# Four convolution taps on VectorE, thirteen pooled key tiles and maxima by accumulators alone, in a two-layer attention kernel

## The reference

```python
g = clip(bn(conv1x1(l, w_inside)), 0, 6)
theta = l[:, :32]
f = einsum('niab,nicd->nabcd', theta, theta)
f = softmax(f.reshape(n, h * w, h, w), axis=1)
f = softmax(f.reshape(n, h * w, h * w), axis=2)
out = einsum('nabcd,nicd->niab', f, g) / h * w
out = bn(conv3x3_depthwise(out, w_dw)) + l
```

## Time and profile before

| | us |
|---|---|
| Median of 3 runs (5228.88 to 5233.55) | 5230.44 |
| Span of the profiled execution | 5229.7 |
| TensorE busy | 5201.4 (99%) |
| ScalarE busy | 5093.6 (97%) |
| GpSimd busy | 4435.3 (85%) |
| VectorE busy | 4411.4 (84%) |

### The profile page before, as it was taken

The page is one execution under the profiler, slowest core; times in us unless marked ns, Lnnn a source line. Parts: engine busy times, 40 slices in busy tenths (PEclk is TensorE's granted clock), DMA queues, the critical chain, the costliest instruction groups (busy, mean ns, idle before and its releaser), DMA issues.

```text
span 5229.7 us, 88157 instructions
## 1 busy us (share of the span) xinstructions
PE 5201.4 (99%) x32196; PEld 2524.0 (48%) x32196; DVE 4411.4 (84%) x8862; ACT 5093.6 (97%) x2949; POOL 4435.3 (85%) x1854
## 2 busy tenths in 40 slices
PE   9999999999999999999999999999999999999999
PEld 3333355444545444545454444545454545444544
DVE  8888888888888888888888888888888888888887
ACT  8888889999999999999999999999999999999998
POOL 7666655998888998888998998899888899888988
PEclk9999999999999999999999999999999999999999
DMA  8898852223222222223232223222222322222122
GB/s 161 169 185 168 164 104 46 48 55 64 55 63 54 55 63 63 63 63 63 63 63 54 47 52 64 59 61 60 48 60 63 63 63 63 63 63 55 43 42 49
DMA packets 226669, 380.19 MB, mean 73 GB/s; under 512 B 158086, under 2 KB 174527, under 8 KB 216128
## 3 DMA queue, kind: packets, MB, share of 16 engines
q1 hardware_dynamic: 225136, 373.67, 34.5%
q10 hardware_dynamic: 1104, 0.89, 0.1%
HBM read 258.82 MB, written 102.74 MB: 69 GB/s over the span
## 4 chain that ended last, share of the span: by engine, by line
PE 83%; ACT 10%; issue 5%; DVE 2%; DMA 0%; SPq 0%; POOL 0%; DVEq 0%
PE at_AV L1302 35%; PE at_S L1261 21%; PE at_AV L1308 10%; ACT at_ring L1044 7%; PE l_TY L612 6%; PE l_TY L619 4%; PE l_SEL L601 3%; ACT at_ring L1050 3%; PE at_AV L1298 2%; DVE at_ring L1117 2%; PE at_AV L1273 0%; DVE at_GT L1177 0%; DVE at_ZACC L1220 0%; DMA l_X<-in_x 0%; DVE at_ACC L1210 0%
## 5 line engine op out<-in xcount | busy, mean ns | idle before, releaser
L1117 DVE TENSOR_SCALAR_CACHE_REDUCE at_ring<-at_S 128x1344 f32<-128x1344 f32 (+2 forms) x2352 | 2882.8, 1242 | 461.2 <-PE at_S L1261 444.3
L992 POOL TENSOR_TENSOR at_ZP<-at_ZP,at_ring 128x1568 f32<-128x1568 f32 x640 | 2268.5, 3581 | 144.4 <-ACT at_ring L1050 134.4
L1302 PE MATMUL at_AV<-at_ring,at_GT 128*64 128x392 f32 x12800 | 2300.3, 500 | 3.8 <-issue 3.7
L1044 ACT ACTIVATE at_ring<-at_ring,at_NM 128x3136 f32<-128x3136 f32 x784 | 2272.6, 2899 | 12.8 <-DVE at_NM L1126 11.8
L1050 ACT ACTIVATE at_ring<-at_ring,at_RZ 128x3136 f32<-128x3136 f32 x784 | 2274.0, 2901 | 0.0
L1302 PEld LDWEIGHTS at_AV<-at_ring,at_GT 128*64 128x64 f32 x12800 | 854.1, 137 | 1143.8 <-issue 1107.6
L1261 PE MATMUL at_S<-at_THM,at_THS 128*128 128x448 f32 x5376 | 1381.7, 387 | 11.6 <-DVE at_ring L1117 9.2
L1261 PEld LDWEIGHTS at_S<-at_THM,at_THS 128*128 128x128 f32 x5376 | 927.1, 188 | 631.6 <-DVE at_ring L1117 291.4
L1013 POOL TENSOR_TENSOR at_OUTB<-at_OUTB,at_ZB 128x1568 f32<-128x1568 f32 x246 | 878.1, 3570 | 16.8
L1308 PE MATMUL at_AV<-at_ring,at_ones 128*32 128x392 f32 x7168 | 676.9, 498 | 2.9 <-DVE at_ACC L1210 2.9
L567 DVE TENSOR_TENSOR l_U<-l_TY,l_XB 128x512 f32<-128x512 f32 x784 | 486.8, 683 | 86.0 <-PE l_TY L612 84.3
(11 more groups left out here) (91 smaller groups left out, 2491.4 us busy)
## 6 DMA issues: line engine op xcount, KB each, us to landing
at_THM<-hld SPq DMA_DIRECT2D x128, 392.0 KB, 6.2
at_THS<-hld SPq DMA_DIRECT2D x256, 192.0 KB, 4.0
l_X<-in_x SPq DMA_DIRECT2D x124, 392.0 KB, 7.2
at_CIN<-att SPq DMA_DIRECT2D x62, 406.0 KB, 7.5
at_ZB<-rzd SPq DMA_DIRECT2D x62, 406.0 KB, 7.8
yd<-l_YO SPq DMA_DIRECT2D x128, 196.0 KB, 5.4
att<-at_ACC SPq DMA_DIRECT2D x248, 98.0 KB
at_OUTB<-yd SPq DMA_DIRECT2D x62, 392.0 KB, 8.5
```

Of the source, the lines that this page charges most:

```text
L992: e.tensor_tensor(z, z, v, ALU.add).then_inc(g_add, 1)
L1044: e.activation(v, v, ACT.Exp, bias=NM[:, i:i + 1], accum_out=ZS[:, i:i + 1]).then_inc(a_p1, 1)
L1117: e.tensor_scalar(ring[:, s % RING, SC * a_:SC * b].rearrange("p (b w) -> p b w", w=SC), PS[:, k % 2, bank:bank + b - a_, 0:SC], 1.0, None ...
L1302: ins = e.matmul(dst[64 * j:64 * j + 64, 0:QC], GT[fl.n % 2][:, keys_of(fl.n, t), :], ring[:, slot, q:q + QC], start=(i == 0), stop=(i == ...
```

## The change

- Taps 0 to 3 of the nine leave GpSimd for VectorE, for all images but the last: `tap` is one `scalar_tensor_tensor` each, `OUTB + w * CIN`. The first waits for step 0 (new semaphore `g_sc`) and for `OUTB`'s load, each other for the one before. GpSimd's first sum (tap 4) waits for the four (`v_cv`). The planner gives a tap rank 3 and 1950 ns.
- Step 1 goes: the bias is added in the product of tap 4.
- `POOL_OF` goes from 2 to 3 in the first two groups: tiles 1 to 6, 8, 9, 12, 13, 16, 17 and 19 are pooled, 13 in all.
- `negmax` goes: the copies negate the scores and take a minimum, the second and third piece with the previous piece's result as second scalar, so the last one leaves the negated maximum in `NM`. Each waits for the one before. The first exponential has scale −1, and waits for `v_m`.

```diff
-POOL_OF = (2, 2, 2, 2, 2, 1, 0)
+POOL_OF = (3, 3, 2, 2, 2, 1, 0)
...
+TAPS = (0, 1, 2, 3)
...
-    conv = [(n, step) for n in range(n_img - 1) for step in range(20)]
+    conv = [(n, step) for n in range(n_img - 1) for step in range(20) if step == 0 or step > 1 and (step - 2) // 2 not in TAPS]
+    taps = [(n, v) for n in range(n_img - 1) for v in TAPS]
...
+        if taps:
+            cv.append((max(td, scaled.get(taps[0][0], inf) + LAT), 3, "tap"))
...
-            cg.append((max(tg, image_end.get(conv[0][0], inf) + 20000), 1, "conv"))
+            n, step = conv[0]
+            first = step == 3 + 2 * next(v for v in range(9) if v not in TAPS)
+            cg.append((max(tg, image_end.get(n, inf) + 20000, tapped.get(n, inf) + LAT if first else 0.0), 1, "conv"))
...
+            elif what == "tap":
+                n, v = taps.pop(0)
+                td = t + 1950
...
-                    link(e.tensor_tensor(CIN[:, :, 1:57], CIN[:, :, 1:57], ZB[:, :, :], ALU.mult))
-                elif step == 1:
-                    e.wait_ge(s_ob, 32 * (n + 1))
-                    link(e.tensor_scalar(OUTB[:, :], OUTB[:, :], 1.0, bq[:, 4:5], ALU.mult, ALU.add))
+                    e.tensor_tensor(CIN[:, :, 1:57], CIN[:, :, 1:57], ZB[:, :, :], ALU.mult).then_inc(g_sc, 1)
+                    e.wait_ge(g_sc, n + 1)
...
-                    link(e.tensor_scalar(T3, CIN[:, i:i + 28, j:j + 56], w9[:, v:v + 1], 0.0, ALU.mult, ALU.add))
+                    link(e.tensor_scalar(T3, CIN[:, i:i + 28, j:j + 56], w9[:, v:v + 1], bq[:, 4:5] if v == TAPS[-1] + 1 else 0.0,
+                                         ALU.mult, ALU.add))
...
+                    if v == TAPS[-1] + 1:
+                        e.wait_ge(v_cv, len(TAPS) * (n + 1))
...
-                e.wait_ge(v_nm, s + 1)
+                e.wait_ge(v_m, NP * (s + 1))
...
-                e.activation(v, v, ACT.Exp, bias=NM[:, i:i + 1], accum_out=ZS[:, i:i + 1]).then_inc(a_p1, 1)
+                e.activation(v, v, ACT.Exp, scale=-1.0, bias=NM[:, i:i + 1], accum_out=ZS[:, i:i + 1]).then_inc(a_p1, 1)
...
+                if c:
+                    e.wait_ge(v_m, m)
+                elif s >= 4:
+                    e.wait_ge(v_m, NP * (s - 3))
+                if s >= 4 and c == NP - 1:
+                    e.wait_ge(a_p1, s - 3)
+                least = NM[:, i:i + 1] if c == NP - 1 else MX[:, i, c:c + 1]
...
-                                PS[:, k % 2, bank:bank + b - a_, 0:SC], 1.0, None, ALU.mult, ALU.max,
-                                accum_out=MX[:, i, c:c + 1]).then_inc(v_m, 1)
...
-                e.tensor_reduce(NM[:, i:i + 1], MX[:, i, :], axis=AX.X, op=ALU.max, negate=True)\
-                 .then_inc(v_nm, 1)
+                                PS[:, k % 2, bank:bank + b - a_, 0:SC], -1.0, MX[:, i, c - 1:c] if c else None, ALU.mult, ALU.min,
+                                accum_out=least).then_inc(v_m, 1)
...
+            def tap(n, v):
+                i, j = divmod(v, 3)
+                if v == TAPS[0]:
+                    e.wait_ge(g_sc, n + 1)
+                    e.wait_ge(s_ob, 32 * (n + 1))
+                else:
+                    e.wait_ge(v_cv, len(TAPS) * n + TAPS.index(v))
+                O3 = OUTB[:, :].rearrange("p (r w) -> p r w", w=W)
+                e.scalar_tensor_tensor(out=O3, in0=CIN[:, i:i + 28, j:j + 56], scalar=w9[:, v:v + 1], in1=O3,
+                                       op0=ALU.mult, op1=ALU.add).then_inc(v_cv, 1)
```

More of the change, by code:

```diff
@@ L172, in plan @@
     adds = [(n, t, h) for n in range(n_img) for t in POOLED for h in range(2)]
-    conv = [(n, step) for n in range(n_img - 1) for step in range(20)]
+    conv = [(n, step) for n in range(n_img - 1) for step in range(20) if step == 0 or step > 1 and (step - 2) // 2 not in TAPS]
+    taps = [(n, v) for n in range(n_img - 1) for v in TAPS]
+    scaled, tapped = {}, {}
     inf = float("inf")
@@ L176, in plan @@
     pe, dve, pool = [], [], []
-    end_s, end_m, end_nm, end_a, end_r, end_p2, group_end, t_fill = {}, {}, {}, {}, {}, {}, {}, {}
+    end_s, end_m, end_a, end_r, end_p2, group_end, t_fill = {}, {}, {}, {}, {}, {}, {}
     end_add, summed, image_end = {}, {}, {}
     tp = ta = td = tg = 0.0
-    n_s = n_m = n_nm = n_r = n_ev = n_a = 0
+    n_s = n_m = n_r = n_ev = n_a = 0
     cur, at, mode = None, 0, 0
@@ L186, in units_at @@
         return end_add.get((f.n, POOLED[-1], f.j), inf) + LAT if t == SUM else 0.0
-    while n_a < 2 * total or main or cur is not None or n_ev < len(fills) or adds or conv:
+    while n_a < 2 * total or main or cur is not None or n_ev < len(fills) or adds or conv or taps:
         t_s = inf
@@ L218, in plan @@
             if n_a == 0:
-                t_a = max(ta, end_nm.get(0, inf) + LAT)
+                t_a = max(ta, end_m.get(NP - 1, inf) + LAT)
             elif n_a == 2 * total - 1:
@@ L222, in plan @@
             elif part == 1:
-                t_a = max(ta, end_nm.get(s + 1, inf) + LAT)
+                t_a = max(ta, end_m.get(NP * (s + 2) - 1, inf) + LAT)
             else:
@@ L228, in plan @@
         cv = []
-        if n_m < NP * total and n_m // NP == n_nm:
+        if n_m < NP * total:
             s = n_m // NP
@@ L237, in plan @@
             cv.append((max(td, end_s.get(piece(n_m)[3], inf) + LAT, free), 2, "M"))
-        elif n_nm < total:
-            cv.append((max(td, end_m[NP * n_nm + NP - 1] + LAT), 0, "nm"))
         if n_r < total:
@@ L304, in plan @@
                 n_m += 1
[L305 to L308, removed]
             elif what == "r":
@@ L312, in plan @@
                 n_r += 1
+            elif what == "tap":
+                n, v = taps.pop(0)
+                td = t + 1950
+                if v == TAPS[-1]:
+                    tapped[n] = td
+                dve.append(("tap", n, v))
             else:
@@ L328, in plan @@
                 tg = t + (3600 if step == 0 or step % 2 and step > 1 else 1620)
+                if step == 0:
+                    scaled[n] = tg
                 pool.append(("conv", n, step))
@@ L686, in build @@
         ZC = sb("ZC", [98, 32])
-        MX = sb("MX", [128, 4, NP])
+        MX = sb("MX", [128, 4, NP - 1])
         NM = sb("NM", [128, 4])
@@ L753, in build @@
         v_wt = sem("vwt")
-        v_nm = sem("vnm")
         v_fin = sem("vfin")
         v_m = sem("vm")
+        v_cv = sem("vcv")
+        g_sc = sem("gsc")
         v_r = sem("vr")
@@ L1061, in _ @@
             e.wait_ge(v_wt, 1)
-            e.wait_ge(g_w, 19 * (last - 1) + 1)
+            e.wait_ge(g_sc, last)
             for k, v in enumerate(HELPED):
@@ L1225, in first_tile @@
                     copy(m)
-                negmax(0)
             l0_vector(e, fold, first_tile)
-            acts = {"M": copy, "nm": negmax, "r": recip, "ev": evacuate}
+            acts = {"M": copy, "r": recip, "ev": evacuate, "tap": tap}
             for n in range(last):
@@ L1238, in _ @@
             acts["lz"] = last_shares
-            for what, *args in dve_order[NP + 1:]:
+            for what, *args in dve_order[NP:]:
                 acts[what](*args)
```

7 lines of the change are left out of this document (removed).

## The result

The changed kernel takes 5400.73 us in the median of four runs (5387.96 to 5412.32), against 5231.29 of the kernel before in the same comparison. The ratio is 1.0323, with an interval of 1.0310 to 1.0335. So it is 169 us slower; 57 were forecast, and the range ended at 5390. The profiled execution's span is 5400.3 us (before: 5229.7).

A forecast was written before the change was run, and what follows sets the result against it. ScalarE was taken to bound the attention stage, with VectorE having to feed it in time. 5229.7 − 4 (TensorE's relief) + 62 (ScalarE standing behind blocked taps) + 1 for the median gave 5288 us, range 5222 to 5390.

The forecast's parts named there:

- What bounds the kernel: Attention stage: ScalarE, 99.98% busy, sets a floor of 784 steps of 5.70 us, 4465 us, that TensorE's relief can't lower.
- TensorE's 87 us of relief: Row-sum matmuls dropped for newly pooled tiles: 2.7 us an image, hidden behind ScalarE, worth 0 to 6 us, taken as 4.
- The accumulators: Maxima taken in VectorE's copies instead of 784 reductions: load 4.89 us a tile, bounds 4.65 to 5.1.
- A tap by itself: One unblocked tap of 1568 elements on VectorE: 1.85 us, four of them 7.4 us an image.
- The standing: A VectorE tap meeting a GpSimd instruction that reads SBUF waits until it ends: 1.4 us a tap on average.
- Slack: Taps put VectorE 5 us behind per image; 3.0 us slack before ScalarE absorbs part, leaving 2 us, 62 in all.
- The upper end, 155 us: Worst end for the taps: each waits 1.79 us, 6.6 us behind against 1.6 of slack, over 31 images.
- The wait for the scaled image: First tap waits for GpSimd's scaling, moved from about 30 to 56 us by two extra pooled tiles; costed at nothing.
- the rival without it: Scaling planned before tile 6, VectorE stands for it: 7 us an image, 217 in all, about 5445 us; chance 0.10.
- at full clock: Expected sign in the profile after: TensorE shows waits for evacuations while its clock stays full; no size given.
- The taps hide: Rival: GpSimd's idle times and scores running ahead hide VectorE's taps, slack exceeds 5 us: 5225 to 5232 us; chance 0.27.
- TensorE's relief pays: Rival: ScalarE only follows TensorE's pace, so 87 us go: 5143 us, or 5220 at best with ScalarE's floor; chance 0.10.

The follow-up runs named there:

- experiments 4: Kernel before with only the accumulator maxima and the bias in a scaled copy; all nine taps on GpSimd, 11 pooled tiles: 5236.32 us (1.0009).
- experiment 7: Changed kernel with the four VectorE taps left out and planned at price 0, so no order is shaped by them; 13 pooled tiles: 5252.39 us (1.0037).
- experiment 2: Changed kernel with each tap replaced by a one-SBUF-input instruction over the same number of elements, nothing added up in OUTB: 5285.72 us (1.0102).
- 9: Changed kernel with full taps, but GpSimd's additions of the pooled tiles replaced by memsets that read nothing: 5287.73 us (1.0110).
- experiment 3: Changed kernel with each tap cut to one element a partition, both SBUF inputs kept: 5298.61 us (1.0128).
- Experiment 8: Changed kernel, complete with taps, but 11 pooled tiles instead of 13: 5625.03 us (1.0748).
- experiments 5: Changed kernel without the four VectorE taps, with dummy matmuls in TensorE's planned idle times: 5299.22 us (1.0127).
- experiment 6: Changed kernel, complete with taps, with dummy matmuls in TensorE's planned idle times: 5405.05 us (1.0329).
- experiment 1: Changed kernel in its own planned order, with the four VectorE taps left out: 5283.84 us (1.0097).
- experiment 10: Changed kernel, complete, with each tap cut into two halves of 14 rows, planned at 1.13 us each: 5528.72 us (1.0579).

## Why the prediction was wrong in size and right in kind

**What bounds the kernel: right.** ScalarE sets the stage. (Its 784 steps give 4465 us at 5.695 us each, and 4469 at the 5.70 written; nothing hangs on it.) TensorE's 87 us of relief are worth nothing: experiments 4 and 7 differ by the two pooled tiles and by 1.8 us, to the wrong side. The forecast had −4.

**The accumulators: right.** 4.89 us a tile was said to be harmless, and it costs 2.2 us in all. The scalar operand adds 1614 − 1551 = 63 ns to a piece; I had 55.

**A tap by itself: right.** 1.85 us was forecast, 1.83 measured.

**The standing: its mechanism right, its size too high.** The forecast had 1.4 us a tap. The mean is 2.881 − 1.83 = 1.05, and half of the taps stand. Mis-sized is the share that meets GpSimd: 75 to 80% were forecast, and 67 of the 124 taps (54%) begin inside one of its instructions, 57 in an addition and 10 in a product. One that does stands 1.94 us on average (130/67), where 1.79 was forecast. The longest tap takes 5.22 us, forecast 5.4. Not quite as forecast is how they end: a tap waits for GpSimd's instruction and then takes its own 1.83 us. In each of the 61 this work begins 0.17 to 0.20 us before a GpSimd instruction ends. Five of them had met an addition at its very end and stood through the whole next one. What it hangs on was taken away from both sides: without the tap's second SBUF input (experiment 2) or without the reads of GpSimd's additions (9), no tap lasts over 1.85 us. The rule of the Trainium skill that I leant on (SBUF — State Buffer, "Who interferes with whom") says just this, and both runs agree with it.

**Slack: this is the step that failed**, "VectorE falls 5 us behind … 5 − 3 = 2 us". With the standing as it was measured the same working gives even less. Four taps cost VectorE 4 x 2.88 = 11.5 us over ten tiles, 60.4 us of work in 57, so 3.4 us behind, and against 3.0 us of slack some 0.4 x 31 = 12 us. Measured were 167.6. Two things were wrong in it.
- *I credited the slack once for each image and against the sum of the four.* The slack isn't a store that is full when a tap comes. In experiment 2, where taps cost what the plan says, the stage is already 52 us longer: the order has used up what there was. From there on most of it counts: 130 us of standing gave 115.5 us of stage, 0.89 of it, and in experiment 3, 38 us beyond the holes gave 20.5. I had taken the slack from the trace of before, whose order has no taps, and used it for an order that has. Nor is a median the right figure for it: from a tile's last copy to its exponential the median over the 784 tiles is 1.7 us in the changed kernel and 1.8 before, and the 94 waits don't show in it.
- *The order itself had no price in my sum.* The planner fills each of VectorE's gaps with a tap of 1950 ns and arranges the evacuations and TensorE's fills around it. It does so greedily, with no regard for ScalarE. By its own costs, with nothing ever standing, its schedule for before leaves ScalarE idle for 1.3 us over the stage, and its schedule for the change for 30.8; for experiment 7 it is 1.1. On the chip this order costs 45.5 us. I read the planner's code for where the taps would fall, and didn't ask what its plan gives to ScalarE.

The upper end, 155 us, came near by errors that cancelled: it had 6.6 us behind where the measured standing gives 3.4, and 1.6 us of slack where there was none to spend.

**The wait for the scaled image: right, and its price too.** In the changed kernel the scaling has no idle time before it in any image:

```profile
L1009 POOL TENSOR_TENSOR at_CIN<-at_CIN,at_ZB x31: 3457/3493/3597, 934.0 to 5292.9; 128x1680 f32<-128x1680 f32 x31
```

It starts 55 us after tile 1's second exponential (56 forecast), and the taps begin 59 to 97 us after it. The cover named was the two extra pooled tiles; the rival without it was priced at 217 us. Experiment 8 takes the cover away and costs 213.

**GpSimd: right.** 79% busy, and no bound. Its first sum now waits for the last tap in ten images, 138.5 us in all. What that cost wasn't separated from the rest.

**TensorE standing "at full clock": wrong**, 171 us of the stage were at 1.2 GHz. No run shows harm from it (experiments 5 to 7).

**The rivals.** "The taps hide" fell: 115.5 us of the stage go when nothing stands. "TensorE's relief pays" fell with experiment 7. My later theory, that the taps are the whole loss, fell with experiment 1, and that of the clock with 5 and 6. None of the eleven is faster than the kernel before. Thirteen pooled tiles with all nine taps on GpSimd weren't run. They would be 24 additions of 3.58 us, two copies of 1.5, the scaling of 3.5 and nine pairs of 1.58 + 3.57, together 138.8 of the 139.7 us that an image takes (24.5 x 5.70).

## What to carry to other kernels

Before a step moves to an engine that feeds the bound one, ask what that engine's instruction shares with others while it runs: an instruction with two SBUF inputs on VectorE stood behind nearly each running GpSimd instruction that read SBUF (61 of the 67 met), inside its own duration, where no view of waits shows it. Compare the shortest duration of a form with its mean. Slack read in one trace belongs to that trace's order; a greedy planner spends it, so take its plan for the new work and look at the bound engine's idle time in it before adding any delay that the plan doesn't know. And where two engines are full in step, compute the other one's floor before relief of the one is counted as won: here 87 us of it won nothing.

## What the runs showed of the hardware that was not expected

- The standing is at most about one GpSimd instruction for each VectorE instruction, however short that is: 3.60 − 0.20 = 3.40 us for one element (experiment 3), 5.22 − 1.83 = 3.39 for 1568, with additions of 3.58. Cutting an instruction in two multiplies the meetings: 323 us of standing against 130 (experiment 10).
- GpSimd pays too. Its additions rose from 3582 ns to 3693 on average in the same stretch, since one that starts under a running tap stands as well. Over the whole trace 67 of the 768 do, and take 4.84 us on average, where the others take 3.58. In experiment 2, with one SBUF input, those that start under a tap take 3.56:

```profile
L1002 POOL TENSOR_TENSOR at_ZP<-at_ZP,at_ring 128x1568 f32<-128x1568 f32 x495 | 1805.6, 3693 | 239.0 <-ACT at_ring L1061 179.7 <-issue 57.1 <-POOL at_OUTB L1024 0.4
```

- No cost of TensorE's lower granted clock was seen where ScalarE sets the pace: the stage of experiment 7 is 4.0 us over before in all, with 75 us of it at 1.2 GHz. In the changed kernel 171 us were, and with the gaps filled and a clock of 0.998 (experiment 6) no time came back.
